# Gathering node rows into two banks, with the row indices staged by VectorE a group ahead

## The chip, the cores and the metric

The kernel runs on one core of a Trainium2 chip. The metric is the device time of one execution in microseconds (us); lower is better. Everything on this page is of that one core. The engines are PE (TensorE), DVE (VectorE), ACT (ScalarE), POOL (GpSimd) and SP (SyncE).

## What is computed

A graph with 12,500 nodes of 128 features and 212,500 directed edges goes through four layers. What matters here is that each layer's message passing is "gather the source node's row, scale it, add it into the destination node's row":

```python
# layer 0, twice: relational convolution, 10 relations
seg  = dst * 10 + edge_type
sums = segment_sum(x[src], seg);  cnt = segment_sum(1, seg)
out  = einsum('nrd,rdo->no', sums / max(cnt, 1), w_rel) + x @ root + bias
# layer 1: 3 relations, scaled per edge
out  = segment_sum(hr[rel_type, src] * norm, dst)
# layer 2, twice: mean over neighbours
out  = (segment_sum(h[src], dst) / max(deg, 1)) @ Wl.T + bl + h @ Wr.T
# layer 3: filter per edge, then segment_sum
agg  = segment_sum(h[idx_j] * Wij, idx_i)
```

The edges come sorted by destination. Between the layers stand a layer norm, relu and dense products on 12,500 x 128 values.

## The kernel before, in words

Edges are laid out in tiles of 128, one edge per partition; a group is 16 tiles (2,048 edges), and there are 104 groups (`ngroups`, `ntiles` = 1,664). A quad is four tiles; four quads make a group. A pass goes once over all groups. There are seven: COUNT (counts edges per relation), then five passes that gather, namely one LOOKUP and four PLAIN, and FILTER. Between passes a dense part (`DENSE`) transforms the nodes with PE and writes a table of rows to DRAM; a gathering pass reads its rows from that table. The outer `reps` loop turns once for this input.

One group of a gathering pass:

- POOL (lines 575 to 591) waits until PE has used up half of the tile `rows` (16 x 128 values a partition), copies eight columns of row indices from `row_i` into `row_st` (line 583), waits for its own copy, and issues eight indirect DMAs (line 588), each of which gathers 128 rows of 512 B from the table into one of the 16 slots of `rows`. Then the same for the other half. `rows` is a single bank: slots 0 to 7 for the next group can be refilled once PE has multiplied quads 0 and 1 of this one, slots 8 to 15 after quads 2 and 3. The count that tells it is the semaphore `mm_done`, one increment per tile.
- DVE (`run_pass`, lines 1009 to 1124) starts a group when `mm_done` says that PE has multiplied all of the group before. It copies the group's offsets and weights to `rw_st` (lines 1015, 1032), then builds 16 matrices of 128 x 128, "weight where the edge's destination is this node" (line 1038; the tile `hot` lies in `tab_s`). It adds each quad's result from PSUM into `acc` (line 997), once `mm_done` has counted the quad.
- PE (`quad_products`, line 726) multiplies quad by quad: four 128 x 128 fp32 products that sum up in PSUM bank `ps[q]` (line 734). It waits for the rows (`row_in[q]`, four gathers of 16 each), for `hot_ready`, and for `add_done` of the group before.

In LOOKUP, each edge's weight is first looked up from a table of reciprocal counts: PE transposes the one-hot relation matrix (line 791), ACT copies it out of PSUM (line 682), PE multiplies it with the table (lines 801, 803), DVE reduces the product with `hot` into the weights (line 1050, twice per tile), and only then is the quad's `hot` ready. So every quad goes round PE, ACT and DVE before its rows are multiplied. The last PLAIN pass also finds the destinations for FILTER: DVE compares the quad's sources with each other (lines 1069, 1080), on index rows that SP loads into `scratch` (line 456).

`scratch` is a wide tile (12,800 values a partition) that other stages use in pieces. In the gathering passes its columns 0 to 6,400 hold LOOKUP's table; columns from 9,216 on are used in FILTER alone (`dst_row`, `nodes`); the last PLAIN pass has `src_row` just below, in 7,168 to 9,215.

A semaphore `row_staged` orders POOL's copy before POOL's gathers; `rows_ready` tells that `row_i` holds the indices for the coming table. At the start of a pass DVE computes the windows of destinations (`set_windows`, lines 975 to 990).

## Time and profile before

| | us |
|---|---|
| median of 3 timed runs | 18279.3 |
| lowest, highest | 18266.46, 18298.8 |
| span of the profiled execution | 18422.2 |
| POOL busy | 11077.2 |
| PE busy (matmul) | 8433.5 |
| DVE busy | 7139.1 |
| ACT busy | 2442.5 |
| five gathering passes, first to last gather of each | 12,660 |

The profiled execution's span is 143 us above the median of the timed runs; its own time beside the span isn't told apart. The five gathering passes lie at 1117 to 3875 (LOOKUP), 4171 to 6599, 6806 to 9235, 9458 to 11893 (PLAIN) and 12014 to 14624 (the PLAIN pass that also finds destinations); the dense parts lie between them, COUNT before and FILTER behind.

How to read it: a timeline row gives the start, the duration, the engine, the source line and what it writes and reads; in square brackets stands how long the engine had been idle before it and what ended that. "issue" means that the profile shows no wait; "remote" means that a semaphore ended the wait whose giver the profile can't name. In the rows PE shows 8 MATMUL records for the 4 fp32 products of a quad.

### The profile page before, as it was taken

What the parts mean: (1) busy time and instruction counts of PE and PEld (TensorE: products, weight loads), DVE (VectorE), ACT (ScalarE), POOL (GpSimd) and SP (SyncE); (2) the same over time, 40 slices, a digit from 0 to 9 for tenths busy, and PEclk for the clock granted to TensorE, in tenths of its full rate; (3) what the DMA queues carried; (4) which work ended last, traced back from release to release, by engine and by line L of the source; (5) the groups of instructions that cost most, each with busy time, mean ns of one, the idle gap of its engine ahead of it and who ended that gap; (6) DMA issues with size and microseconds to landing.
All of it is one profiled execution on the core that took longest, in us unless ns stands there. A gap on an engine that the chain in (4) does not pass through costs nothing. (4 is left out here: it accounts for less than half of the span.)

```text
span 18422.2 us, 189911 instructions
## 1 busy us (share of the span) xinstructions
PE 8433.5 (46%) x37745; PEld 6706.7 (36%) x37746; DVE 7139.1 (39%) x33414; ACT 2442.5 (13%) x4374; POOL 11077.2 (60%) x11347
## 2 busy tenths in 40 slices
PE   2464444463333343333343333333333377777777
PEld 1233333333333333333332332322222355555555
DVE  7644444432222232222232222255555534444443
ACT  0120000020000020000020000000000044444443
POOL 0045555636666646666636666566666448888883
PEclk9975555585555565555565555555555567777775
DMA  2131111131111131111121111123333246666665
GB/s 85 64 123 40 40 39 39 40 146 55 45 45 45 45 100 45 45 45 45 45 66 45 45 45 45 49 80 84 83 84 84 73 95 118 118 117 118 117 117 122
DMA packets 981246, 1326.79 MB, mean 72 GB/s; under 512 B 201421, under 2 KB 635620, under 8 KB 981180
## 3 DMA queue, kind: packets, MB, share of 16 engines
q0 software_dynamic: 552016, 851.84, 21.1%
q1 hardware_dynamic: 429208, 474.72, 8.9%
q8 instruction: 6, 0.10, 0.0%
q14 instruction: 16, 0.13, 0.0%
HBM read 992.21 MB, written 333.54 MB: 72 GB/s over the span
## 5 line engine op out<-in xcount | busy, mean ns | idle before, releaser
L588 POOL DMA_INDIRECT rows<-table_dram,row_st x8320 | 8018.1, 964 | 3188.8 <-issue 2894.6
L734 PE MATMUL ps<-tab_s,rows 128*128 128x128 f32 x16640 | 4123.4, 427 | 6939.1 <-DMA rows<-table_dram,row_st 4302.8
L734 PEld LDWEIGHTS ps<-tab_s,rows 128*128 128x128 f32 x16640 | 3604.2, 320 | 7432.5 <-issue 7386.0
L570 POOL DMA_INDIRECT agg_dram<-acc,sum_row x1664 | 2646.9, 1591 | 529.0 <-issue 383.7
L997 DVE TENSOR_TENSOR acc<-ps,acc 128x128 f32 x2080 | 605.5, 291 | 5685.4 <-PE ps L734 4010.6
L1038 DVE TENSOR_SCALAR tab_s<-iota,rw_st 128x128 f32<-128x128 f32 x6656 | 1787.8, 361 | 11.5
L734 PE MATMUL ps<-scratch,tab_s 128*128 128x128 f32 x3328 | 669.0, 366 | 821.8 <-DVE scratch L1182 791.5
L583 POOL COPY row_st<-row_i 128x8 int32 x1040 | 210.5, 202 | 1262.7 <-PE ps L734 1072.4
L734 PEld LDWEIGHTS ps<-scratch,tab_s 128*128 128x128 f32 x3328 | 596.8, 269 | 871.7 <-issue 871.3
L548 POOL DMA_DIRECT2D table_dram<-tab_s x200 | 106.6, 533 | 1179.9 <-ACT tab_s L671 917.4
L635 ACT ACTIVATE yT<-acc 128x512 f32 x75 | 46.9, 626 | 4899.5 <-DVE acc L997 4893.7
L1176 DVE COPY sum_row<-etype 128x4 int32 x416 | 81.3, 195 | 1458.4 <-POOLq L569 1400.8
L1050 DVE CUSTOM_DVE_ANT_0 xs<-ps,tab_s 128x128 f32<-128x128 f32 x1664 | 385.1, 287 | 629.2 <-remote 446.2
L825 PE MATMUL ps<-scratch,acc 128*128 128x128 f32 x3328 | 593.3, 338 | 10.1 <-issue 5.9
L682 ACT ACTIVATE yT<-ps 128x512 bf16<-128x512 f32 x416 | 248.4, 597 | 2519.3 <-remote 1111.3
L1069 DVE TENSOR_SCALAR xn_h<-scratch,src_st 128x128 f32<-128x128 int32 x1664 | 377.5, 299 | 517.9 <-remote 392.0
L752 PE MATMUL ps<-scratch,wfilt 20*128 20x512 f32 x836 | 553.1, 745 | 35.0 <-DMA scratch<-in_feat 27.7
L825 PEld LDWEIGHTS ps<-scratch,acc 128*128 128x128 f32 x3328 | 559.2, 253 | 17.4 <-issue 17.4
L1050 DVE CUSTOM_DVE_ANT_0 tab_s<-ps,tab_s 128x128 f32<-128x128 f32 x1664 | 384.6, 287 | 457.5 <-remote 389.8
L551 POOL DMA_DIRECT2D table_dram<-tab_s x100 | 75.5, 755 | 795.6 <-ACT tab_s L671 609.7
L760 PEld LDWEIGHTS ps<-wfilt,scratch 128*128 128x128 f32 x3336 | 510.4, 219 | 15.8
L760 PE MATMUL ps<-wfilt,scratch 128*128 128x128 f32 x3336 | 507.3, 302 | 0.0
(182 smaller groups left out, 10596.4 us busy)
## 6 DMA issues: line engine op xcount, KB each, us to landing
scratch<-in_src_row SPq DMA_DIRECT2D x832, 256.0 KB
rows<-table_dram,row_st POOLq DMA_INDIRECT x8320
table_dram<-tab_s POOLq DMA_DIRECT2D x200, 640.0 KB, 3.2
scratch<-in_dst_row SPq DMA_DIRECT2D x416, 256.0 KB
scratch<-table_dram SPq DMA_DIRECT2D x416, 64.0 KB
agg_dram<-acc,sum_row POOLq DMA_INDIRECT x1664
scratch<-agg_dram SPq DMA_DIRECT2D x100, 256.0 KB, 3.8
x_dram<-xn_h SPq DMA_DIRECT2D x75, 256.0 KB, 2.4
```

Source lines behind the costliest of these rows:

```text
L570: pool.indirect_dma_start(agg_dram[j], bass.IndirectOffsetOnAxis(ap=sum_row[:, QUAD * q + j:QUAD * q + j + 1], axis=0), sums[:, q, j * P:( ...
L583: pool.tensor_copy(row_st[:, us[0]:us[-1] + 1], row_i[:, bass.ds(g * GROUP + us[0], GROUP // 2)]).then_inc(row_staged, 1)
L588: pool.indirect_dma_start(rows[:, u, :], None, table_dram[p["rels"]], bass.IndirectOffsetOnAxis(ap=row_st[:, u:u + 1], axis=0)).then_inc(r ...
L682: act.activation(rel_hotT[:, q % 2, :], ps[4][:], ACT.Copy).then_inc(relT_ready, 1)
L734: pe.matmul(o, lhs[:, u, :], rhs[:, u, :], start=j == 0 or not summed, stop=j == QUAD - 1 or not summed).then_inc(mm_done, 1)
L752: pe.matmul(ps[4][:], wfilt1[:], feat[:, q, :], start=True, stop=True).then_inc(f1_mm, 1)
L760: mm = pe.matmul(ps[6 + b][:, j * P:(j + 1) * P], f_buf[:, 2, b, j * P:(j + 1) * P], W["wfilt2"][:], start=False, stop=j == QUAD - 1)
L825: mm = pe.matmul(ps[5][:, j * P:(j + 1) * P], hotT[:, q % 2, j * P:(j + 1) * P], nodes[:, q % 2, :], start=True, stop=True)
L997: dve.tensor_tensor(window, ps[q][0:m, 0:P], window, ALU.add).then_inc(add_done, QUAD)
L1038: dve.tensor_scalar(hot[:, u, :], iota[:], rw_st[:, 0, u:u + 1], rw_st[:, 1, u:u + 1], ALU.is_equal, ALU.mult).then_inc(hot_ready, 1)
L1050: dve.tensor_tensor_reduce(out=out, in0=looked_up, in1=hot[:, u, :], scale=1.0, scalar=0.0, op0=ALU.mult, op1=ALU.add, accum_out=wout_st[: ...
L1069: i = dve.tensor_scalar(pairs[:, j, :], src_row[:, q, j * P:(j + 1) * P], src_st[:, u:u + 1], None, ALU.is_equal)
```

## The change

A second bank of 16 tiles is laid into `scratch` (columns 9,216 to 11,263). Even groups gather into `rows`, odd groups into this bank, each with its own four semaphores `row_in`; the loops over groups are written out for two groups a turn (`groups_by_bank`), on POOL, PE and DVE. POOL no longer copies indices: it waits once per group for `row_staged` and once for `mm_done` (all of the group two before, which is the last user of this bank), then issues all 16 gathers. The indices of group g+1 are copied by DVE to one half of a doubled `row_st`, as the first thing of its group g, behind its wait for the end of group g-1 on PE; those of group 0 are copied at the start of a pass, behind `set_windows`. `row_i` gets 16 more columns, for the copy past the last group. `mm_done` starts at two groups instead of one, and each wait for it is moved by one group. What each engine multiplies, adds and gathers stays as it is.

```diff
+        row_banks = [rows, scratch[:, rows_at:rows_at + GROUP * P].rearrange("p (u c) -> p u c", u=GROUP)]
-        row_st = sb("row_st", [P, GROUP], I32)
+        row_st = sb("row_st", [P, 2, GROUP], I32)
-        row_in = [sem(f"row_in{q}") for q in range(4)]
+        row_in = [[sem(f"row_in{b}{q}") for q in range(4)] for b in range(2)]
+        def groups_by_bank(e, body):
+            with e.Fori(0, ngroups // 2) as i:
+                body(i * 2, 0, i)
+                body(i * 2 + 1, 1, i)
+            if ngroups % 2:
+                body(ngroups - 1, 0, ngroups // 2)
                 with pool.Fori(0, reps) as r:
-                    with pool.Fori(0, ngroups) as g:
+                    def gather(g, bank, i):
                         turn = pool.snap(reps * (k * ngroups) + r * ngroups + g)
                         used = pool.snap(reps * ntiles + turn * GROUP)
-                        for part in range(2):
-                            pool.wait_ge(mm_done, used + (part + 1) * (GROUP // 2))
-                            us = range(part * (GROUP // 2), (part + 1) * (GROUP // 2))
-                            pool.tensor_copy(row_st[:, us[0]:us[-1] + 1],
-                                             row_i[:, bass.ds(g * GROUP + us[0], GROUP // 2)]).then_inc(row_staged, 1)
-                            pool.wait_ge(row_staged, turn * 2 + (part + 1))
-                            settle(pool)
-                            for u in us:
+                        pool.wait_ge(row_staged, (reps * k + r) * (ngroups + 1) + g + 1)
+                        pool.wait_ge(mm_done, used + GROUP * (3 - apart))
+                        settle(pool)
+                        for q in range(4):
+                            for u in range(QUAD * q, QUAD * (q + 1)):
                                 pool.indirect_dma_start(
-                                    rows[:, u, :], None, table_dram[p["rels"]],
-                                    bass.IndirectOffsetOnAxis(ap=row_st[:, u:u + 1], axis=0)
-                                ).then_inc(row_in[u // QUAD], 16)
+                                    row_banks[bank][:, u, :], None, table_dram[p["rels"]],
+                                    bass.IndirectOffsetOnAxis(ap=row_st[:, bank, u:u + 1], axis=0)
+                                ).then_inc(row_in[bank][q], 16)
+                    groups_by_bank(pool, gather)
...
             for q in range(4):
-                                gathered(landed, q)
+                                gathered(landed, bank, q)
...
+                    if kind != COUNT:
+                        dve.wait_ge(rows_ready, sum(q in (0, 2, 3) for q in range(pn)))
+                        dve.tensor_copy(row_st[:, 0, :], row_i[:, 0:GROUP]).then_inc(row_staged, 1)
...
-                        dve.wait_ge(mm_done, base + GROUP)
+                        dve.wait_ge(mm_done, base + 2 * GROUP)
+                        if kind != COUNT:
+                            staged_next(g, bank)
...
+                    def staged_next(g, bank):
+                        dve.tensor_copy(row_st[:, 1 - bank, :], row_i[:, bass.ds((g + 1) * GROUP, GROUP)]
+                                        ).then_inc(row_staged, 1)
```

## Rows read from the trace of the kernel before

**Rows 1.** The page: span, and section 1 (busy us, share, instructions).

```profile
span 18422.2 us, 189911 instructions
PE 8433.5 (46%) x37745; PEld 6706.7 (36%) x37746; DVE 7139.1 (39%) x33414; ACT 2442.5 (13%) x4374; POOL 11077.2 (60%) x11347
```

**Rows 2.** Busy time by stretch: LOOKUP, the first PLAIN, the last PLAIN pass.

```profile
1117.00:3875.00 2758.00, 1164.83 (x7034) 994.02 (x7034) 1340.42 (x9423) 247.76 (x415) 1650.09 (x1871) 0.58 0.15 40
4171.00:6599.00 2428.00, 845.97 (x3320) 737.75 (x3320) 594.78 (x2291) 0.00 (x0) 1635.44 (x1871) 0.50 0.17 45
...
12014.00:14624.00 2610.00, 845.93 (x3312) 736.22 (x3312) 1422.62 (x7772) 0.00 (x0) 1661.61 (x1871) 0.50 0.30 83
```

The columns of rows 2 are: the stretch, its length, then busy us (instructions) of PE, PEld, DVE, ACT and POOL, PE's granted clock, the share of the DMA engines, GB/s.

**Rows 3.** The page's costliest groups of POOL: busy, mean ns, idle before.

```profile
L588 POOL DMA_INDIRECT rows<-table_dram,row_st x8320 | 8018.1, 964 | 3188.8 <-issue 2894.6
L583 POOL COPY row_st<-row_i 128x8 int32 x1040 | 210.5, 202 | 1262.7 <-PE ps L734 1072.4
```

**Rows 4.** POOL's waits by stretch: LOOKUP, first PLAIN, last PLAIN (us, times, longest).

```profile
POOL row_st L583 <- PE ps L734: 434.5, 89, 8.6
...
POOL row_st L583 <- PE ps L734: 134.9, 40, 3.7
...
POOL row_st L583 <- PE ps L734: 240.3, 63, 7.0
```

**Rows 5.** Timeline, 8000 to 8050, in the middle PLAIN pass.

```profile
8007.79 2.04 PE L734 MATMUL ps<-tab_s,rows 128*128 128x128 f32 x8 [3.81 <-DVE tab_s L1038]
...
8011.91 0.97 POOL L588 DMA_INDIRECT rows<-table_dram,row_st  x1 [0.81 <-issue]
...
8020.72 0.95 POOL L588 DMA_INDIRECT rows<-table_dram,row_st  x1 [0.30 <-issue]
8022.16 0.29 DVE L997 TENSOR_TENSOR acc<-ps,acc 128x128 f32 x1 [11.82 <-remote]
...
8023.49 2.05 PE L734 MATMUL ps<-tab_s,rows 128*128 128x128 f32 x8 [3.00 <-DMA rows<-table_dram,row_st]
...
8025.16 0.19 POOL L583 COPY row_st<-row_i 128x8 int32 x1 [3.49 <-PE ps L734]
...
8037.81 2.04 PE L734 MATMUL ps<-tab_s,rows 128*128 128x128 f32 x8 [2.96 <-DMA rows<-table_dram,row_st]
...
8039.99 0.29 DVE L997 TENSOR_TENSOR acc<-ps,acc 128x128 f32 x1 [4.71 <-PE ps L734]
```

**Rows 6.** Timeline, 3508 to 3541, in LOOKUP.

```profile
3529.95 0.95 POOL L588 DMA_INDIRECT rows<-table_dram,row_st  x1 [0.30 <-issue]
3530.30 0.60 ACT L682 ACTIVATE yT<-ps 128x512 bf16<-128x512 f32 x1 [8.00 <-remote]
3530.38 0.29 DVE L1050 CUSTOM_DVE_ANT_0 tab_s<-ps,tab_s 128x128 f32<-128x128 f32 x1 [3.49 <-remote]
...
3533.42 0.60 ACT L682 ACTIVATE yT<-ps 128x512 bf16<-128x512 f32 x1 [2.53 <-PE ps L791]
...
3535.49 0.19 POOL L583 COPY row_st<-row_i 128x8 int32 x1 [4.59 <-PE ps L734]
...
3540.79 0.17 DVE L1015 COPY rw_st<-rel_dst 128x16 f32 x1 [0.98 <-issue]
```

**Rows 7.** DVE's longest waits in LOOKUP (us in total, times, longest).

```profile
DVE tab_s L1050 <- remote: 385.5, 127, 4.9
```

**Rows 8.** Timeline, 12800 to 12860, in the last PLAIN pass.

```profile
12809.40 0.08 DVE L1080 DVE_READ_ACCUMULATOR2_ANT dup<- 128x1 f32 x1 [1.12 <-issue]
...
12813.69 1.00 DVE L1069 TENSOR_SCALAR xn_h<-scratch,src_st 128x128 f32<-128x128 int32 x4 [4.21 <-issue]
```

**Rows 9.** Timeline, the starts of two PLAIN passes.

```profile
4170.18 0.19 POOL L583 COPY row_st<-row_i 128x8 int32 x1 [3.37 <-DMA table_dram<-tab_s]
...
4173.64 0.15 DVE L988 TENSOR_SCALAR win<-win 128x1 f32<-128x1 f32 x1
...
6804.41 10.72 DVE L1286 MEMSET acc<- 128x12800 f32 x1 [2.62 <-issue]
```

More of the change, by code:

```diff
@@ L555, in _ @@
                 wait_stores(pool, k)
-                if PASSES[k + 1] != FILTER:
-                    pool.wait_ge(rows_ready, sum(q in (0, 2, 3) for q in range(k + 1)))
-                else:
+                if PASSES[k + 1] == FILTER:
                     with pool.Fori(0, reps) as r:
@@ L771, in run_pass, with group @@
                         settle(pe)
-                    with pe.Fori(0, ngroups) as g:
+                    def group(g, bank=0, i=0):
+                        rows = row_banks[bank]
                         base = pe.snap(reps * (pn * ntiles) + r * ntiles + g * GROUP)
@@ L832, in run_pass @@
                                 quad_products(base, q, same, P, msg, summed=False)
+                    if kind in (LOOKUP, PLAIN):
+                        groups_by_bank(pe, group)
+                    else:
+                        with pe.Fori(0, ngroups) as g:
+                            group(g)
             run_pass(0)
@@ L1124, in run_pass @@
                                 dve.tensor_tensor(part, wout_st[:, w, :], part, ALU.add)
+                    def staged_next(g, bank):
+                        dve.tensor_copy(row_st[:, 1 - bank, :], row_i[:, bass.ds((g + 1) * GROUP, GROUP)]
+                                        ).then_inc(row_staged, 1)
+                    if kind == COUNT:
+                        with dve.Fori(0, ngroups) as g:
+                            group(g)
+                    else:
+                        groups_by_bank(dve, group)
             def filter_pass():
```

32 lines of the change are left out of this document (18 added, 14 removed).

## The prediction

> **What bounds the kernel now.** I read the page first: a span of 18422.2 us, and POOL the busiest engine at 60% [rows 1]. Then the busy times by pass. Each gathering pass lasts 2428 to 2758 us, with POOL busy some 1640 of it, PE 850 to 1160 and DVE 590 to 1420; the passes not shown, the second and third PLAIN, are like the first (2429 and 2435 us) [rows 2]. So no engine fills a pass by its busy time. But a gather costs POOL more than its 964 ns [rows 3]: the next never starts sooner than 0.30 us after it [rows 5]. 8320 gathers at 0.964 + 0.30 are 10,517 us, against 12,660 for the five passes. POOL's issue of gathers is thus 83% of them, and 2143 us are left for whatever else holds it. The rest of the span (COUNT, the dense parts, FILTER) isn't touched.
>
> Where the 2143 go, from POOL's own groups: it waits 1262.7 us before the 1040 index copies, for PE to free a half; the copies take 210.5 [rows 3]; and the first gather behind a copy comes 0.81 us after it where others come after 0.30 [rows 5], which is 1040 x 0.51 = 530. That is 2003; the other 140 are some 80 long gaps of the gathers themselves. The waits by pass: 434.5 for PE in LOOKUP, 134.9 in the first PLAIN pass, 240.3 in the last [rows 4].
>
> The next question is why POOL waits at all in PLAIN. PE needs 2.05 us per quad, some 8 us per group, against 16 x 1.26 = 20.2 us of gathering. The timeline shows it. The quad at 8007.79 is done at 8009.83, yet DVE's add for it starts at 8022.16, after 11.82 idle us, and POOL, which also waits for PE's counts, gets on at 8025.16, 3.49 us after its last gather ended [rows 5]. The same pair takes 0.14 us one group later: PE ends at 8039.85, the add starts at 8039.99 [rows 5]. So an increment that PE, DVE or ACT gives is sometimes seen at once and sometimes many us late, and the late ones come while a long run of gathers is under way. LOOKUP, which hands every quad round three engines, shows it best. DVE at 3530.38 waits only for its own results of 3.49 us before, ACT at 3530.30 had stood 8.00 us, both while POOL gathers (3529.95); once POOL has stopped, ACT follows PE shortly (3533.42) [rows 6]. In this pass that kind of wait sums to 385.5 us for one of DVE's lines alone, 127 times [rows 7]. In the last PLAIN pass DVE even stands inside a line, 1.12 us at 12809.40, and 4.21 us at 12813.69 with no wait that the profile names [rows 8]. I don't know what delays these increments; I take from the rows that uninterrupted gathering goes with it and a pause of POOL ends it.
>
> **The change part by part.** (a) Index copies leave POOL: -210.5 us, and the 0.51 us after each of them, -530; in their place come two waits and a settle per group, whose cost between two gathers no row shows. From below it is nothing (POOL's sequencer may run ahead), from above the 0.51 of a copy's hand-over, so 520 x 0 to 0.51 = 0 to 265; I take the middle, 130, being nearest to neither row. (b) The waits for a free half go: up to -1262.7. (c) DVE gets 520 + 5 copies. Its own of this kind take 0.17 to 0.19, so some 95 us, at the start of a group where DVE is otherwise first in the chain; in PLAIN POOL's gathers cover them, and in the two heavy passes they cost up to 208 x 0.17 = 35. (d) DVE's copy is queued behind its wait for the end of the group before on PE and behind that group's four adds. POOL waits for it. Today POOL waits for PE directly, and for half a group. (e) At a pass's start the copy stands behind `set_windows`: POOL's first copy was at 4170.18, DVE is free at 4173.64, so +4 us in four passes, and one pass clears `acc` before (10.72 us from 6804.41), +15 [rows 9]: +31 in all. (f) The moved `mm_done` thresholds and the bank's place in `scratch` cost nothing: no stage of these passes touches the columns. FILTER and COUNT keep their waits, only with other constants.
>
> If (b) came in full, each pass would be bound by POOL's issue: -2003 + 130 + 31 = -1842. What is late next decides. A group's work on DVE, PE and ACT now has to fit into 20.2 us, while gathers run without the pause. In PLAIN it is short (hot matrices 4.2 us, quads 8 us, adds 2 us), rows land about 2.8 us after the last gather's start (8020.72, PE at 8023.49) [rows 5], and with the second bank increments may come up to 14 us late before POOL misses them. So I give PLAIN its gain in the first three passes: per pass 154 us of waits, 41 of copies and 208 x 0.51 = 106, less 26 for the new boundary, 275; times three, 825.
>
> In LOOKUP I give none. POOL now restarts (3535.49) 5.3 us before DVE starts the next group (3540.79) [rows 6]; afterwards it can start only with DVE. The stretch of gathering then lies later in the group's chain: it ends some 22.5 us after DVE's start, where it now ends after 18.7. In those 3.8 us a step (DVE, PE or ACT waiting for one another) takes up to 4 us instead of 1.2, a loss of up to 2.7 us per group; against it stand up to 0.7 us, the copies' pauses. Between -0.7 and +2.7 I take +1.0, that is +104. The last PLAIN pass has the same shape (13.5 us of DVE work per group, stands of 4 us [rows 8]) and I give it the same, +104, with -0.7 to +4 as bounds. The sum: -825 + 104 + 104 + 31 = -586, and from the median of 18279.3 that is 17,693. The profiled execution's span would go from 18422 to about 17,836; I assume that a gain carries over from it to the timed runs one to one.
>
> One rule speaks against (c). The Trainium skill, page "SBUF — State Buffer", section "Who interferes with whom", says that a DVE copy can hold a port that GpSimd needs to write its descriptors, and the loser stands for the whole instruction. The rows show POOL's gathers at 0.95 to 0.97 us next to DVE's work [rows 5], so little of it. By that rule 520 copies could each hold POOL for their 0.17 us, 90 us in all, which my range covers.
>
> **The rivals.** (A) POOL bound throughout: the late increments are a result of the half-bank waits, or harmless once there are two banks. All of 1842 us comes, 16,437. For it: 2003 us stand there plainly, and LOOKUP's chain has run in under 20 us at times. Against it: rows 6 to 8, where the late steps are on DVE and ACT, which don't wait for POOL at all. 0.15.
>
> (B) My forecast: PLAIN gains, the two heavy passes don't. 0.40; between -900 and 0.
>
> (C) Slower: the pauses that go are what lets the increments through. Then PE's counts of a group stay behind until POOL has used up what it may gather. POOL stops after 32 gathers, the counts come 3.5 us later [rows 5], and now DVE must still do four adds (2 us) and its loop's start (1 us) and the copy before POOL goes on: some 7 us of pause in place of 3.5. In PLAIN, once in two groups, (40.4 + 7) / 2 = 23.7 us per group against 23.35 now, +110 over three passes. In LOOKUP +1.5 and in the last pass +2 us per group, the middle of their bounds or a little above it, +364. With +31: 18,785. It decides from the point where PE's counts come more than some 14 us late in PLAIN; the 11.8 us seen is near. For it: LOOKUP shows quick steps only with POOL stopped. 0.37, and up to 18,950 and beyond.
>
> (D) No change, because the passes are bound by something that carries gathers and increments together and doesn't care how they are ordered: 18,280. The three like passes, 2428, 2429 and 2435 us, would fit. 0.08.
>
> **How the numbers follow.** Faster by over 0.2% (about 37 us, what a measurement of this kernel can tell from no change): all of A and most of B, 0.53. Within 0.2%: D, 0.08. Slower: C and the end of B, 0.39. The likeliest case gives the time, 17,690; its own range is 17,380 to 18,280. The range that should hold the time 8 times in 10 goes from 16,500, which leaves out about half of A, to 18,950, which leaves out the far part of C.
>
> **What would show it.** In the changed kernel's trace POOL's copies are gone and its idle time sits before the first gather of a group. Step (b) is right in PLAIN if the passes take 2130 to 2170 us and the gap at a group's first gather is mostly under 0.8 us; wrong if every second one is some 7 us. LOOKUP tells A (about 2160 us) from B (2860) and C (2910). If DVE's and ACT's "remote" waits in LOOKUP shrink though POOL gathers without a pause, the late increments were not what I think. The prediction fails if the increments come early enough in LOOKUP (far below), or too late in PLAIN (above 18,279).

## The result and the profile after

The changed kernel takes 19264.28 us, median of 4 runs (19264.07 to 19280.99), against 18278.44 us for the kernel before (4 runs, 18266.46 to 18298.8): a ratio of 1.0546, 95% interval 1.0534 to 1.0559. It is 986 us slower. The forecast of 17,690 us missed on the side of rival C.

That is not the whole result. The same two kernels, timed against each other again in a later session, gave 16334.43 us (2 runs, 16320.57 to 16348.29) against 17217.67 us (9 runs, 17196.68 to 17224.08): a ratio of 0.949, interval 0.9462 to 0.9517, or 883 us faster. In that session the kernel before is itself 1,061 us faster. Traces of that session show what differs: the counts (semaphore increments) that engines give each other arrive at once, also while POOL gathers. There are two conditions, then. I call them late counts and prompt counts; every session showed one of them in all its kernels:

| session | kernel before, us | counts | what ran in it |
|---|---|---|---|
| result | 18,278 | late | the changed kernel: 19,264 |
| 1 | 18,262 | late | own copies, one count per quad (twice), short pause |
| 2 | 17,198 | prompt | old waits, staging with old waits, long pause, SyncE's loads |
| 3 | 17,218 | prompt | the changed kernel: 16,334; old waits, staging with old waits, SyncE's loads |
| 4 | 17,198 | prompt | staging with old waits, SyncE's loads, long pause |
| 5 | 17,196 | prompt | first mixed kernel |
| 6 | 18,410 | late | second mixed kernel |
| 7 | 18,268 | late | staging with old waits, own copies in one pass |

The sessions ran on chips with different numbers; sessions 1 and 3 have the same number and different conditions, sessions 2 and 5 share another number and were both prompt. What makes the condition is not known.

The page of the changed kernel, in the session of the result (before: rows 1). POOL's work fell by 253 us and the span rose all the same. PE's busy time fell by 358 us for the same 37745 records; its granted clock was higher in part of the passes (0.57 against 0.50 in the first PLAIN, below):

```profile
span 19279.3 us, 185757 instructions
## 1 busy us (share of the span) xinstructions
PE 8075.9 (42%) x37745; PEld 6491.0 (34%) x37746; DVE 7152.1 (37%) x33940; ACT 2442.5 (13%) x4374; POOL 10824.7 (56%) x10307
...
L596 POOL DMA_INDIRECT scratch<-table_dram,row_st x4160 | 4009.1, 964 | 3329.0 <-DVE row_st L1152 1755.3 <-issue 1573.4 <-PE ps L744 0.3
L596 POOL DMA_INDIRECT rows<-table_dram,row_st x4160 | 3974.2, 955 | 2193.3 <-issue 1964.3 <-DVE row_st L1152 229.0
```

A gather costs what it did (964 and 955 ns) [rows 3]. POOL's idle time before gathers and copies was 3188.8 + 1262.7 = 4452 us and is now 5522 us. The same two groups with prompt counts have 2587 us, which is little more than 0.30 us for each of 8320 gathers:

```profile
L596 POOL DMA_INDIRECT rows<-table_dram,row_st x4160 | 4004.6, 963 | 1319.7 <-issue 1244.1 <-DVE row_st L1152 74.8 <-PE ps L744 0.9
L596 POOL DMA_INDIRECT scratch<-table_dram,row_st x4160 | 3989.1, 959 | 1267.6 <-issue 1267.3 <-DVE row_st L1152 0.3
```

Busy times by stretch, columns as in rows 2, from the first to the last gather of a pass. The changed kernel with late counts: LOOKUP, first PLAIN, last PLAIN:

```profile
1142.00:4366.00 3224.00, 1241.95 (x6983) 1054.03 (x6983) 1317.37 (x9438) 245.37 (x411) 1595.33 (x1664) 0.55 0.13 34
4684.00:7179.00 2495.00, 694.44 (x3320) 638.31 (x3320) 598.05 (x2389) 0.00 (x0) 1593.01 (x1664) 0.57 0.17 44
...
12720.00:15476.00 2756.00, 843.24 (x3296) 733.85 (x3296) 1407.78 (x7821) 0.00 (x0) 1608.01 (x1664) 0.50 0.29 79
```

and with prompt counts:

```profile
1140.00:3247.00 2107.00, 1064.77 (x7064) 928.86 (x7064) 1329.26 (x9564) 248.37 (x416) 1600.14 (x1664) 0.65 0.20 52
3547.00:5645.00 2098.00, 849.01 (x3320) 738.82 (x3320) 591.18 (x2391) 0.00 (x0) 1590.27 (x1664) 0.50 0.21 52
...
10404.00:12529.00 2125.00, 849.24 (x3320) 739.06 (x3320) 1393.80 (x7899) 0.00 (x0) 1617.28 (x1664) 0.50 0.39 102
```

Against rows 2, LOOKUP went from 2758 to 3224 us, PLAIN from 2428 to 2495, the last from 2610 to 2756; the five passes together from 12,660 to 13,455 us (first gather to last), and the stretches between and before them grew by 57 us. The rest of the 986 is that the profiled execution of before was 144 us above its median, and that of the changed kernel 15. With prompt counts every pass takes about 104 x 20.2 us, that is 16 gathers of 1.26 us per group and nothing else.

Below I give each kernel as us per group in its five passes: from the first gather of a pass's first group to that of its last, by 103.

| kernel | LOOKUP | PLAIN 1, 2, 3 | last PLAIN | whole, us |
|---|---|---|---|---|
| before, late | 26.6 | 23.4, 23.4, 23.4 | 25.1 | 18,278 |
| changed, late | 31.1 | 24.0, 24.0, 24.0 | 26.6 | 19,264 |
| before's schedule (old waits), prompt | 22.0 | 22.0, 21.9, 22.0 | 22.3 | 17,218 |
| changed, prompt | 20.3 | 20.2, 20.2, 20.2 | 20.4 | 16,334 |

The first row comes from that execution 144 us above the median. The kernel before with one count for four (below), at 18,275 us and with late counts, has 26.2, then 23.2, 23.3, 23.2, then 24.6, so the first row may be up to 0.5 us too high.

Where the time goes with late counts is in the timeline of the changed kernel, 8000 to 8060, in the middle PLAIN pass (compare rows 5):

```profile
8007.22 2.05 PE L744 MATMUL ps<-tab_s,scratch 128*128 128x128 f32 x8 [0.38 <-DMA scratch<-table_dram,row_st]
...
8012.42 2.04 PE L744 MATMUL ps<-tab_s,scratch 128*128 128x128 f32 x8 [3.16 <-DMA scratch<-table_dram,row_st]
...
8017.45 2.05 PE L744 MATMUL ps<-tab_s,scratch 128*128 128x128 f32 x8 [2.98 <-DMA scratch<-table_dram,row_st]
...
8026.69 0.29 DVE L1015 TENSOR_TENSOR acc<-ps,acc 128x128 f32 x1 [14.43 <-remote]
...
8034.77 0.95 POOL L596 DMA_INDIRECT rows<-table_dram,row_st  x1 [0.30 <-issue]
8040.69 0.72 DVE L1015 TENSOR_TENSOR acc<-ps,acc 128x128 f32 x2 [13.71 <-remote]
8042.21 0.17 DVE L1152 COPY row_st<-row_i 128x16 int32 x1 [0.80 <-issue]
...
8043.35 1.00 POOL L596 DMA_INDIRECT scratch<-table_dram,row_st  x1 [7.63 <-DVE row_st L1152]
...
8043.93 6.00 PE L744 MATMUL ps<-tab_s,rows 128*128 128x128 f32 x32 [24.44 <-DVE tab_s L1062]
```

PE has finished the group's last quad at 8019.50 and the one before it at 8014.46. DVE can add these two only at 8040.69, 21 and 26 us later and 4.97 us after POOL's last gather has ended (8035.72). Then come DVE's adds, its loop's start and its copy, and POOL goes on after 7.63 us. The second quad's add is late too (its products end at 8009.27, the add starts at 8026.69), but it starts while POOL gathers. So a pause isn't the only way through. The trace's own record of `mm_done` shows both: its updates come singly, 3 to 7 us apart, while POOL gathers, and the last five within 0.2 us, at 8040.5. In the first PLAIN pass 215 of 416 adds start more than 1.5 us after their products' end, 109 of them inside a run of gathers. In LOOKUP it is 212, of which only 11 inside a run. The same step with prompt counts, in the first PLAIN pass:

```profile
5002.45 2.04 PE L744 MATMUL ps<-tab_s,scratch 128*128 128x128 f32 x8 [2.92 <-DMA scratch<-table_dram,row_st]
5003.51 0.95 POOL L596 DMA_INDIRECT rows<-table_dram,row_st  x1 [0.30 <-issue]
5004.72 0.29 DVE L1015 TENSOR_TENSOR acc<-ps,acc 128x128 f32 x1 [4.67 <-PE ps L744]
```

PE ends at 5004.49, DVE adds at 5004.72, 0.23 us later, with POOL gathering all the while. There no add of the first PLAIN pass starts more than 0.8 us after its products. In LOOKUP (late counts; from the view of 3010 to 3030) the group's steps stand together until POOL has stopped:

```profile
3013.86 2.05 PE L744 MATMUL ps<-tab_s,scratch 128*128 128x128 f32 x8 [1.49 <-remote]
3024.34 0.29 DVE L1074 CUSTOM_DVE_ANT_0 xs<-ps,tab_s 128x128 f32<-128x128 f32 x1 [13.14 <-remote]
...
3026.57 0.60 ACT L692 ACTIVATE yT<-ps 128x512 bf16<-128x512 f32 x1 [16.34 <-remote]
...
3027.30 0.29 PE L812 MATMUL ps<-scratch,sel_deg 128*128 x1 [11.39 <-ACT yT L692]
```

POOL's last gather ran from 3022.78 to 3023.73 and its next starts at 3035.12. So of this group's 31 us (POOL began its gathers at 3003.79) some 12 pass with quick steps, 8.4 with DVE, PE and ACT all idle (3015.91 to 3024.34), and 11 again with quick steps, while POOL stands. DVE's and ACT's waits of the kernel whose giver the profile can't name (us in total, times, longest), late:

```profile
DVE acc L1015 <- remote: 4701.7, 524, 20.0
...
DVE xs L1074 <- remote: 1337.4, 107, 21.4
DVE acc L1015 <- PE ps L744: 925.3, 642, 10.9
...
ACT yT L692 <- remote: 1649.0, 119, 33.8
```

and prompt, where no "remote" wait is left on any engine:

```profile
DVE acc L1015 <- PE ps L744: 5433.3, 1267, 8.1
...
ACT yT L692 <- PE ps L802: 1867.7, 416, 17.1
```

Counts are not all that is held back. In the last PLAIN pass of the changed kernel DVE also stands inside a run of its own instructions, with no wait that the profile names (late counts):

```profile
DVE dup L1104 <- issue: 163.2, 187, 1.8
```

Standstills of over 0.6 us of this kind, inside one DVE operation, number 50 to 104 in the last PLAIN pass of every kernel that ran with late counts, and none in any with prompt counts. So the condition touches more than semaphores; I keep the name for what costs the time here.

### The profile page after: what moved, and what is told of

Same layout as the page of the kernel before. It is cut to its first block, busy times and chain, and to the rows that moved or that the text cites. A ratio compares the mean times of both kernels' runs of the same rounds, so it can differ in the third digit from the quotient of the medians.

```text
span 19279.3 us, 185757 instructions
## 1 busy us (share of the span) xinstructions
PE 8075.9 (42%) x37745; PEld 6491.0 (34%) x37746; DVE 7152.1 (37%) x33940; ACT 2442.5 (13%) x4374; POOL 10824.7 (56%) x10307
## 4 chain that ended last, share of the span: by engine, by line
another core or an unknown queue 34%; DVE 18%; issue 15%; PE 12%; DMA 10%; POOL 6%; DVEq 3%; ACT 2%; POOLq 0%; ACTq 0%; SPq 0%
DMA agg_dram<-acc,sum_row 8%; PE ps L744 7%; DVE tab_s L1062 5%; POOL agg_dram L581 4%; POOL scratch L596 2%; DVE xn_h L1093 2%; DVE xn_h L1104 2%; DVE tab_s L1068 2%; PE ps L909 2%; DVE acc L1015 1%; PE ps L867 1%; DVE tab_s L1065 1%; DVEq L328 1%; DMA table_dram<-tab_s 1%
## 5 line engine op out<-in xcount | busy, mean ns | idle before, releaser
L596 POOL DMA_INDIRECT scratch<-table_dram,row_st x4160 | 4009.1, 964 | 3329.0 <-DVE row_st L1152 1755.3
L596 POOL DMA_INDIRECT rows<-table_dram,row_st x4160 | 3974.2, 955 | 2193.3 <-issue 1964.3
L744 PE MATMUL ps<-tab_s,rows 128*128 128x128 f32 x8320 | 1773.1, 397 | 4959.1 <-DVE tab_s L1062 4363.4
L744 PEld LDWEIGHTS ps<-tab_s,rows 128*128 128x128 f32 x8320 | 1639.8, 301 | 5093.5 <-issue 5090.0
L744 PE MATMUL ps<-tab_s,scratch 128*128 128x128 f32 x8320 | 1997.7, 420 | 2710.6 <-DVE tab_s L1062 1179.7
L744 PEld LDWEIGHTS ps<-tab_s,scratch 128*128 128x128 f32 x8320 | 1757.3, 313 | 2915.9 <-issue 2827.8
L812 PE MATMUL ps<-scratch,sel_deg 128*128 x416 | 119.9, 288 | 1341.1 <-ACT yT L692 733.9
L762 PE MATMUL ps<-scratch,wfilt 20*128 20x512 f32 x836 | 555.0, 747 | 28.7 <-DMA scratch<-in_feat 23.4
L812 PEld LDWEIGHTS ps<-scratch,sel_deg 128*128 128x128 bf16 x416 | 44.9, 108 | 1436.8 <-issue 1436.1
```

Source lines behind the costliest of these rows:

```text
L596: pool.indirect_dma_start(row_banks[bank][:, u, :], None, table_dram[p["rels"]], bass.IndirectOffsetOnAxis(ap=row_st[:, bank, u:u + 1], ax ...
L744: pe.matmul(o, lhs[:, u, :], rhs[:, u, :], start=j == 0 or not summed, stop=j == QUAD - 1 or not summed).then_inc(mm_done, 1)
L762: pe.matmul(ps[4][:], wfilt1[:], feat[:, q, :], start=True, stop=True).then_inc(f1_mm, 1)
```

## The experiments

The theory, T: in the late condition, it is GpSimd's gathers issued back to back that hold back the counts of TensorE, VectorE and ScalarE, most of them until they pause; the change took the pauses away and hung POOL's restart on DVE. Rivals: R1, only the way over DVE costs; R2, the bank's place in `scratch`; R3, the loops written out for two groups; R4, the number of increments.

### Own copies (late counts)

```diff
+pool.wait_ge(rows_ready, ...)          # once, at the start of a pass
...
-pool.wait_ge(row_staged, ...)
 pool.wait_ge(mm_done, used + GROUP * (3 - apart))
+pool.tensor_copy(row_st[:, bank, :], row_i[...]).then_inc(row_staged, 1)
+pool.wait_ge(row_staged, turn + 1)
```

(and no copy by DVE)

> The changed kernel with both banks, but GpSimd copies its own 16 row indices once per group and waits only for TensorE's products of two groups back; VectorE stages nothing. In the changed kernel GpSimd sees counts about 5 us after its last gather has ended, and with VectorE's adds (about 2 us), its loop start (about 1 us) and its copy ahead of it pauses 7.6 us in every second PLAIN group and about 6 us in each last-PLAIN group. Theory T (the counts of TensorE, VectorE and ScalarE arrive late while gathers are issued back to back, and the way over VectorE is only the end of the pause): the pause falls by the 2.5 to 3 us of VectorE's part, less 0.9 us for its own copy, so PLAIN 24.0 -> 22.7 to 23.2 us per group, LOOKUP 31.1 -> 29 to 31, and the whole 18,600 to 19,000 us, no less. Rival R1 (only the detour over VectorE costs; the counts are in time): no pause is left, 21.0 us per group in PLAIN, and the whole comes to 17,000 us or below.

Measured: 18,759 us (before on the same chip 18,262); 30.0, 23.3, 23.3, 23.3 and 25.0 us per group. POOL's waits (us in total, times, longest):

```profile
POOL row_st L594 <- PE ps L747: 1161.3, 155, 13.3
...
POOL row_st L594 <- remote: 789.0, 196, 5.8
```

T's whole fits, its PLAIN was 0.1 us too low. With DVE out of POOL's way 505 of the 986 us come back, but 481 don't: R1 alone falls, as half of the cause it stands. What POOL still waits for here is PE's counts of two groups back.

### One count for four (late counts)

```diff
-    pe.matmul(...).then_inc(mm_done, 1)
+    mm = pe.matmul(...)
+mm.then_inc(mm_done, QUAD)
```

(likewise `hot_ready`, `hot_made` and the counts of the dot products)

> The changed kernel with one semaphore increment per four products, per four one-hot tiles and per four dot products in the place of four (and one per sixteen one-hot tiles in the place of sixteen); nothing else differs. Rival R4 (each increment is served slowly while gathers are issued, so their number makes the lag): a quarter of them cures most of it, LOOKUP 31.1 -> 26 us per group or less, the whole 17,000 to 18,300 us. Theory T (what is held back is held until the gathering pauses, whatever the number): within 100 us of the changed kernel's 19,264 us.

> The same edit on the kernel before: one increment for four products, one-hot tiles and dot products. R4: the wait of 3.5 us at a group's start and TensorE's lags shrink, 17,300 to 18,000 us. T: within 100 us of the kernel before's 18,278 us.

Measured: 19,249 us on the changed kernel, 15 below its result, and 18,275 us on the kernel before, 12 above the one beside it. R4 falls: the number of counts doesn't matter. In the changed kernel with one count per quad, a quad whose products ended at 8008.30 was still added only at 8023.40, by a single count.

### A short pause (late counts)

```diff
+if q == 2:
+    pool.tensor_copy(idle_st[:], iota_i[:, 0:8]).then_inc(idled, 1)
+    pool.wait_ge(idled, turn + 1)
```

> The changed kernel, and after 8 of a group's 16 gathers GpSimd makes one small copy into an unused tile and waits for that copy's own count (about 1.2 us in which it issues no gather). It adds work and a wait for nobody. Theory T: held-back counts pass in the pause, so the LOOKUP group falls from 31.1 to 28 to 30 us, the last PLAIN from 26.6 to 25 to 26, PLAIN stays within 0.7 of 24.0, and the whole falls to 18,700 to 19,200 us. The rival, under which counts are in time and GpSimd's own path sets the end: each of the 416 groups gets longer by up to 1.2 us, the whole rises to 19,300 to 19,760 us.

Measured: 19,040 us; 30.2, 23.7, 23.6, 23.6 and 26.3 us per group. POOL does 520 copies more and stands 0.7 us longer at each, and the kernel gets 224 us faster. The whole is as T said; its LOOKUP and last PLAIN were each 0.2 to 0.3 us above T's bounds, so 0.7 us lets less through than I thought.

### Old waits, staging with old waits, long pause, SyncE's loads (met prompt counts)

The old waits, and the same with DVE's staging (there without the copy):

```diff
-pool.wait_ge(row_staged, ...)          # kept in the one with staging
-pool.wait_ge(mm_done, used + GROUP * (3 - apart))
...
+if q % 2 == 0:
+    pool.wait_ge(mm_done, used + (GROUP + (q // 2 + 1) * half))
+    pool.tensor_copy(row_st[...half...], row_i[...]).then_inc(row_staged, 1)
```

> The changed kernel with its two banks, its loops written out for two groups and its larger tiles, but GpSimd keeps the waits of the kernel before: two halves per group, each after TensorE's same half of the group just before, and each with GpSimd's own copy of 8 indices; VectorE stages nothing. Only the time at which gathers may start is put back. Theory T (it is the uninterrupted gathering that costs): the kernel before's time, 18,180 to 18,380 us, groups of 26.6, 23.4 and 25.1 us. Rivals R2 (the bank in scratch costs) and R3 (the longer loops cost): a good part of the +986 us stays, 18,600 us or more.

> As the run with the old waits, but VectorE stages the 16 indices as in the changed kernel, so GpSimd has only the two waits per group on TensorE's halves. Theory T: the staging is over before either wait ends, and the two copies of 0.7 us leave GpSimd, but the pause between the halves, in which counts pass, goes with them: 18,000 to 18,450 us. Rival R1 (the dependence of GpSimd on VectorE's queue is what costs): 18,700 us or more.

The long pause is the short one five times over. SyncE's loads, in LOOKUP and the first three PLAIN passes, take consecutive rows; the kernel leaves out the gathering by index, so its time is not one of the whole computation:

```diff
+for u in range(GROUP):
+    sp.dma_start(row_banks[bank][:, u, :], table_dram[p["rels"]][u * P:(u + 1) * P, :]
+                 ).then_inc(loads_in[bank][u // QUAD], 16)
```

> The changed kernel with a pause of five small copies by GpSimd, each waited for (about 3.5 to 4 us in all), after 8 of the 16 gathers; one such copy made the gap 0.7 us longer and took 224 us off. Theory T: three to four us are enough for the held-back counts of TensorE, VectorE and ScalarE to arrive in the middle of the group, so the LOOKUP group falls from 31.1 to 26 to 28.5 us, the last PLAIN to 24.5 to 26, PLAIN stays at 23.5 to 24.5, and the whole comes to 18,300 to 18,900 us, below the 19,040 us of the short pause. The rival, under which GpSimd's own path sets the end and the short pause helped by something else: up to 3.7 us more for each of 520 groups, 20,000 us or more.

> The changed kernel in which, in LOOKUP and the first three PLAIN passes, SyncE loads 16 tiles of 128 consecutive rows per group by plain DMA, under the same waits, in the place of GpSimd's 16 gathers; what is left out is the gathering by index (the rows are the table's first 2,048), so the time is not one of the whole computation. The bytes into SBUF, the packets' size and all the other engines' work stay; GpSimd is idle in these passes, and the last PLAIN pass is as it was. Theory T (GpSimd's issue of gathers is what holds the other engines' counts back): the engines follow each other within 0.1 us, LOOKUP 31.1 -> 20 us per group or less, PLAIN 24.0 -> 12 or less. Rival R5 (the writes of rows into SBUF, or the engines' own chain, hold them): LOOKUP stays at 26 us or more, and the pauses of 10 to 16 us before VectorE's and ScalarE's steps stay.

Measured, with the kernel before at 17,198 us: 17,206 us with the old waits, 16,331 with staging and old waits, 17,478 with the long pause, 12,104 with SyncE's loads. All expectations had been written for late counts, and the times of T and of its rivals for the first three kernels were missed alike. Only what doesn't depend on late counts was settled. Banks and written-out loops cost nothing with prompt counts (R2 and R3 fall there; below with an interval). With late counts no run has them alone; the PLAIN passes of two runs further down, which have both, are no longer than those of before. The long pause costs (17,478 - 16,334) / 520 = 2.2 us per group, with the changed kernel's time from session 3: a pause costs a kernel that POOL bounds, as the rival had it (up to 3.7 us). With late counts pauses made it faster. And SyncE's loads gave the engines' own chain: 16.2 us per group in LOOKUP, 8.1 in PLAIN. So it isn't the other engines' own work that makes a group longer than POOL's 20.2 us.

### The changed kernel again (prompt counts)

> The changed kernel itself. The kernel before took 18,262 us on the chip of the first four experiments and 17,198 us on that of the next four, where the traces show no late counts: GpSimd gathers without a pause in every pass (groups of 20.3 us with VectorE's staging, 22.0 us with its own copies). Theory T2 (lateness of counts under gathering is a property of the chip on which the program runs, and the change loses only where it is there): if the kernel before takes about 17,200 us here, the changed one takes 16,330 to 16,450 us (POOL-bound, as with the old waits and VectorE's staging); if it takes about 18,270 us here, the changed one takes 19,250 to 19,290 us. The rival (the changed kernel's longer run of gathers makes the counts late anywhere): 17,500 us or more on either.

> The kernel of the earlier run with the old waits, on this chip: two banks and loops written out for two groups, GpSimd's waits and copies as in the kernel before. T: within 80 us of the kernel before's time on either kind of chip. R2 and R3 (bank in scratch, longer loops): 300 us or more above it.

> The kernel of the earlier run in which VectorE stages the indices and GpSimd keeps the old waits by halves on the group just before. Where the kernel before takes 17,200 us: 16,330 us as there. Where it takes about 18,270 us: theory T says that the wait for the group before is what gives the counts time to pass, 18,000 to 18,450 us; rival R1 (the dependence on VectorE's queue costs): 18,700 us or more.

> The kernel in which SyncE loads 16 tiles of consecutive rows per group in LOOKUP and the first three PLAIN passes and GpSimd gathers nothing there (the gathering by index is left out). Where the kernel before takes 17,200 us: 12,100 us, groups of 16.1 and 8.2 us. Where it takes about 18,270 us: T (GpSimd's gathers, and nothing else, make counts late) says the same groups of 16.1 and 8.2 us to within 0.5 us, and only the last PLAIN pass is longer, 12,100 to 12,900 us in all; the rival (that chip's counts or engines are slow whatever GpSimd does): LOOKUP 20 us or more per group.

Measured, with the kernel before at 17217.67 us: the changed kernel 16334.43 (ratio 0.949); old waits 17217.88 (8 runs, ratio 0.9999, interval 0.9988 to 1.0011); staging with old waits 16332.84 (0.9489, 0.9461 to 0.9516); SyncE's loads 12109.9. T2's numbers were right; that the chip decides is not, since session 1 had late counts on the same number. The whole gain of 5.1% comes from DVE's staging, which takes two copies and two hand-overs per group from POOL; the second bank and its later wait add nothing to it, since 16,334 and 16,333 are the same.

Staging with old waits, SyncE's loads and the long pause ran once more, in session 4:

> VectorE stages, GpSimd keeps the two waits by halves on the group just before. Where the kernel before takes about 18,270 us (late counts): theory T says 18,000 to 18,450 us, since the waits give the counts time to pass; rival R1 (GpSimd's dependence on VectorE's queue costs) says 18,700 us or more. Where the kernel before takes about 17,200 us: 16,330 us, and it tells nothing new.

> SyncE loads consecutive rows in LOOKUP and the first three PLAIN passes, GpSimd gathers nothing there (the gathering by index is left out). Where the kernel before takes about 18,270 us: T (GpSimd's gathers make the counts late) says groups of 16.1 and 8.2 us as in the other condition, within 0.5 us, and 12,100 to 12,900 us in all, with the last PLAIN pass, which still gathers, the only longer one; the rival (counts are late there whatever GpSimd does) says LOOKUP at 20 us per group or more. Where before takes about 17,200 us: 12,110 us.

> The changed kernel with five small copies by GpSimd, each waited for, after 8 of 16 gathers (the gap is 2.1 us longer). Where the kernel before takes about 18,270 us: T says that it is faster than with one copy (19,040 us): LOOKUP 27 to 29.5 us per group, last PLAIN 24.5 to 26, the whole 18,400 to 18,950 us; the rival (GpSimd's own path) says 2.1 us more for each of 520 groups, 20,000 us or more. Where before takes about 17,200 us: 17,480 us, which is the rival's sum there.

Counts were prompt again: 16,318, 12,102 and 17,460 us, with 17,198 before, as in session 2.

### One kernel with several ways

To compare several ways in one session, each pass got its own. With SyncE's loads in some passes neither time is one of the whole computation.

```diff
+by_sync, by_halves, by_pause = (0, 3), (1, 4), (2,)    # first mixed kernel
+by_sync, by_halves, by_pause = (1,), (0, 3), (2,)      # second; the last PLAIN is as changed
```

> One kernel with a different way in each gathering pass, all with VectorE's staging. LOOKUP and the third PLAIN: SyncE's loads of consecutive rows, no gathers (their gathering by index is left out). First PLAIN and last PLAIN: GpSimd keeps the waits by halves on the group just before. Second PLAIN: the changed kernel's wait and the pause of five small copies. Where the kernel before takes about 18,270 us: T says 16.1 us per group in LOOKUP, 8.2 in the third PLAIN, 22 to 23.5 in the first PLAIN (against 24.0 changed, 23.4 before), 23 to 24.5 in the second and 24 to 26 in the last; the rival that counts are late there whatever GpSimd does says LOOKUP at 20 us or more; R1 (the dependence on VectorE's queue) says first and last PLAIN at 24.0 and 26.6 us as in the changed kernel. Where the kernel before takes about 17,200 us: 16.1, 20.2, 22.3, 8.2 and 20.4 us per group.

> As the mixed kernel before it, with the ways dealt out anew, all with VectorE's staging: LOOKUP and the third PLAIN keep the waits by halves on the group just before, the first PLAIN has SyncE's loads of consecutive rows (its gathering by index is left out), the second PLAIN the pause of five small copies, the last PLAIN is the changed kernel's. Where the kernel before takes about 18,270 us: T says 26 to 27.5 us per group in LOOKUP (31.1 changed, 26.6 before), 8.2 in the first PLAIN, 23 to 24.5 in the second, 22 to 23.5 in the third, 26.6 in the last; R1 says 31 in LOOKUP and 24.0 in the third PLAIN; the rival that counts are late whatever GpSimd does says 12 us or more in the first PLAIN. Where the kernel before takes about 17,200 us: 20.3, 8.2, 22.3, 20.2 and 20.4 us per group.

The first met prompt counts (before 17,196): 14,834 us, 16.2, 20.2, 22.4, 8.1 and 20.2 us per group, all within 0.2 us of what was expected. The second met late counts (before 18,410): 17,173 us. Its five passes:

```profile
1138.00:4020.00 2882.00, 1064.13 (x7026) 921.18 (x7026) 1341.91 (x9514) 247.21 (x414) 1605.32 (x1664) 0.61 0.15 38
4323.00:5161.00 838.00, 525.95 (x3296) 499.03 (x3296) 584.51 (x2372) 0.00 (x0) 0.00 (x0) 0.85 0.46 130
5386.00:7840.00 2454.00, 728.14 (x3296) 665.23 (x3296) 592.70 (x2374) 0.00 (x0) 1688.71 (x2184) 0.56 0.18 44
8063.00:10479.00 2416.00, 807.13 (x3320) 714.73 (x3320) 601.55 (x2390) 0.00 (x0) 1582.91 (x1664) 0.52 0.18 45
10595.00:13365.00 2770.00, 842.81 (x3296) 733.67 (x3296) 1422.31 (x7820) 0.00 (x0) 1600.24 (x1664) 0.50 0.30 78
```

The second row says most about the mechanism. POOL is idle (0.00), SyncE loads the same bytes under the same waits at three times the rate (130 GB/s against 44), and a group takes 838 / 104 = 8.1 us, as with prompt counts, in the middle of a kernel whose other passes have late ones. Its timeline has DVE 0.6 us idle before an add where it stood 14 us:

```profile
4700.72 5.47 PE L775 MATMUL ps<-tab_s,rows 128*128 128x128 f32 x32 [3.14 <-DVE tab_s L1094]
4703.38 7.45 SPq L474 DMA_DIRECT2D scratch<-table_dram  x16
...
4706.40 0.29 DVE L1047 TENSOR_TENSOR acc<-ps,acc 128x128 f32 x1 [0.60 <-PE ps L775]
```

None of DVE's waits in this pass is "remote", and no add starts more than 1.8 us after its products. So counts are late under POOL's gathers, and not under transfers into SBUF as such. One thing is left: SyncE's loads differ from the gathers in the engine that issues them and also in that their rows are consecutive and always the same. No run had POOL load consecutive rows, so which of the two holds the counts back is not shown. The other rows, from a session whose kernel before took 0.7% more than in the result: LOOKUP with staging and the old waits 27.8 us per group, 3.3 less than the changed kernel and a little above T's 27.5 (R1 said 31); the third PLAIN, likewise, 23.3 (R1 said 24.0); the second PLAIN with the long pause 23.6, 0.4 less than without, though POOL works more; the last, unchanged from the changed kernel, 26.7, as in the result.

### Staging with old waits, and own copies in one pass (late counts)

```diff
+if k != 2 and q % 2 == 0:
+    pool.wait_ge(mm_done, used + (GROUP + (q // 2 + 1) * (GROUP // 2)))
...
```

(and POOL's own copies, as above, for k == 2, the second PLAIN pass)

> VectorE's staging with GpSimd's waits by halves on the group just before in LOOKUP and in the first, third and last PLAIN pass; in the second PLAIN GpSimd copies its own 16 indices and waits for the products of two groups back, as in the run with own copies. The output is whole. Where the kernel before takes about 18,270 us or more (late counts): T says 27.8, 23.3, 23.3, 23.3 and 25 to 26 us per group in the order of the passes, and the whole within 200 us of the kernel before on the same chip. Where it takes about 17,200 us: 20.3, 20.2, 21.0 (16 gathers of 1.26 us and one copy of 0.7 to 0.8 us), 20.2 and 20.4 us per group, and 16,410 us in all.

Measured: 18435.97 us (2 runs) against 18268.31, ratio 1.0092, interval 1.0063 to 1.0121. By pass:

```profile
1139.00:3976.00 2837.00, 1087.08 (x7026) 935.83 (x7026) 1346.81 (x9514) 247.59 (x414) 1604.74 (x1664) 0.61 0.15 38
4276.00:6671.00 2395.00, 808.12 (x3320) 714.57 (x3320) 602.78 (x2390) 0.00 (x0) 1597.08 (x1664) 0.52 0.18 46
6900.00:9300.00 2400.00, 627.49 (x3296) 601.42 (x3296) 597.06 (x2368) 0.00 (x0) 1592.17 (x1750) 0.61 0.18 45
9522.00:11919.00 2397.00, 806.40 (x3320) 713.94 (x3320) 602.54 (x2391) 0.00 (x0) 1585.32 (x1664) 0.52 0.18 45
12035.00:14627.00 2592.00, 837.31 (x3304) 728.94 (x3304) 1413.74 (x7848) 0.00 (x0) 1600.17 (x1664) 0.51 0.32 84
```

The last pass takes 25.0 us (25.1 before), PLAIN with staging 23.0 (23.4), PLAIN with own copies 23.3, LOOKUP 27.3 (26.6). T had said 25 to 26, 23.3, 23.3 and 27.8, and its bound of 200 us over the kernel before holds. (The third row begins 22 us behind that pass's first gather, at 6878.) With the wait on the group just before in four passes and own copies in the fifth, 828 of the 986 us come back. Of the 168 us that are left LOOKUP has some 80, 0.8 us per group against the profile of before, or some 120 against the kernel before with one count for four. The short hand-over between the halves, which is missed there, may be why; the loops written out for two groups may be too, since no run has them alone with late counts. Neither is shown. What own copies cost with prompt counts was not met by any run.

Staging with the old waits in all passes is the version I would keep: 16,333 us with prompt counts, the changed kernel's gain in full. With late counts it was not run whole; the mixture above is 0.9% over the kernel before, where the changed kernel is 5.5% over it.

## Why the prediction was wrong

- **What bounds the kernel, and the late counts.** Right, and the base of all else: POOL's issue of gathers, 83% of the passes, and counts of other engines that are late under an uninterrupted run of gathers. The second mixed kernel shows that in a PLAIN pass without these gathers no count is late. One reading was loose: the pair that takes 0.14 us "one group later" is that group's second quad, and its first was prompt as well (products end at 8034.86, add at 8034.99), after seven gathers in a row. So a long run of gathers doesn't hold back every count. What no row could tell is that the lateness is no fixed property: the same kernel has it in some sessions and not in others, and 1,061 us hang on it.
- **(a) Copies leave POOL, -740, a new boundary, +130.** The boundary costs nothing: gathers go from one group to the next at 1.26 us from start to start, as inside a group. With prompt counts this step is all of the gain, against the old waits' schedule: 22.0 - 20.2 = 1.8 us per group, more than the 740 / 520 = 1.4 of the sum. Part of the rest is that POOL's gathers have 90 gaps of 1.7 us with the old waits and none with staging: gaps like these are the sum's "some 80 long gaps", which I had left where they were.
- **(b) The waits for a free half go: the step that failed.** I gave PLAIN its full 825 us because counts may come 14 us late before POOL misses them. They came 21 us late (8019.50 to 8040.69), and those of the quad before 26 us. The lag has no amount of its own: counts that don't get through singly wait for the next pause of POOL, and the second bank moved that pause from 8 gathers away to 32. The allowance of 14 us was held against a lag measured under the old pauses, and against one that wasn't the longest: in the three PLAIN passes of before, 188 of 1,248 adds start over 10 us after their products' end, the latest 14.6 us. The idle time in rows 4 that I had called removable was also time in which counts got through: added pauses made the changed kernel faster (224 us by 0.7 us of pause), and the wait on the group just before brought PLAIN back to 23.0. PLAIN took 24.0 us per group where my sum makes it 20.7 ((2428 - 275) / 104), a miss of some 1,000 us over three passes.
- **(c) DVE's copies.** 0.17 us each, as said. The rule of the Trainium skill ("SBUF — State Buffer", "Who interferes with whom"), by which they could hold POOL's descriptor writes, would have added up to 90 us. No sign of it in the traces: with prompt counts a group is 16 x 1.26 us with the copy in it.
- **(d) POOL hangs on DVE's queue.** Named, but priced in rival C alone. It is real with late counts, 505 us by the own copies, and nothing with prompt ones.
- **(e) Pass starts, +31.** 57 us in the result's trace; with prompt counts the changed kernel's starts lie 33 us later than with the old waits.
- **LOOKUP, +1.0, and the last pass, +1.0 us per group.** The sign was right, the size not: +4.5 and +1.5. The bound of +2.7 in LOOKUP came from 3.8 us of longer gathering in which steps take 4 us instead of 1.2. In fact the steps don't get slow, they stop, for 8.4 us in the group shown. Against the kernel before with one count for four the growth is 4.9 and 2.0.
- **Rival C.** This is what happened. In PLAIN it holds almost to the number: every second group has a pause of 7.6 us (7 said), 24.0 us per group (23.7 said). Its sum, 18,785, is 480 us short, of which LOOKUP is 3.0 x 104 = 312. I gave it 0.37 against 0.40 for the forecast, on the strength of the 14 us.
- **Rival A.** Under prompt counts it is exact in kind: POOL-bound in all passes, 16,334 us (16,437 said), though from a kernel before at 17,218, so its gain is 883 us and not 1,842.
- **Rival D (no change).** It happened in neither condition.
- **The loops, doubled.** With prompt counts, old waits with the written-out loops are the kernel before to 0.1%, so doubling the loops costs nothing there. The Trainium skill, page "Runtime: NRT & Kernel Launch", section "Instruction fetch mechanics", says that a taken branch out of the engine's current window of instructions stalls it; the prediction held that the doubled loop fits into the window, and these runs agree. With late counts it wasn't tried alone.
- **The signs named.** LOOKUP's length was to tell A from B from C by 2160, 2860 and 2910 us; it was 3224 with late counts and 2107 with prompt ones. "Every second gap some 7 us" was the sign against step (b), and it is what the trace has.

## What to carry to other kernels

An idle time that a change removes may be doing work: before its cost is put down as a gain, ask what happened in it, here that other engines' counts arrived. A lag seen in a trace is measured under the pauses of that trace; if the change moves the pauses, work out the lag anew from the mechanism instead of holding it against a slack. And a result on one chip in one session can have its sign from a condition of the session: the run of the kernel before beside it, and a "remote" wait in the profile, tell which one it was.

## What the runs showed of the hardware

- In four of the eight sessions counts of TensorE, VectorE and ScalarE reached a waiting engine late, by 21 and 26 us in the group shown, while GpSimd issued indirect DMAs every 1.26 us. In the changed kernel VectorE's next instruction started, in the median of the groups with a pause, 5.15 us after the last gather had ended in PLAIN and 2.7 us after it in the two other passes. In the other four they took 0.2 us under the same gathers at the same 0.96 us each. Rows loaded by SyncE at 130 GB/s held nothing back in a session with late counts. In the four late sessions VectorE also stood for 0.6 to 1.8 us inside single operations of the last PLAIN pass, 50 to 104 times a kernel; in the others never. Why, and what makes the condition, stays open; no run was made on it beyond these.
- The number of increments has no part in it: a quarter of them changed the time by less than 0.1%.
- A group of gathers that needs no copy by GpSimd starts 1.26 us after the gather before it, across a loop's end and two waits that are already met: they cost nothing.
- TensorE's granted clock over a PLAIN pass was 0.50, the lower of its two levels (1.2 GHz), with groups of 20.2 us, and 0.85 with groups of 8.1 us, where TensorE was busy for 63% of the pass instead of 40%. Eight product records took 2.05 us in the one; in the other 32 took 5.47, that is 1.37 for eight.
